# Two more transposed tiles per block copied by ScalarE, and VectorE's small work regrouped, in a two-layer graph network on one core

## What is computed

```python
# layer 0, h = relu(layernorm(x)), adj is 2048 x 2048, int32, 0 or 1
mask = (adj > 0)
deg = sum(mask, axis=1)
agg = mask @ h / max(deg, 1)
combined = concat([h @ W_self + b_self, agg @ W_nb + b_nb])
x = x + relu(combined @ W_comb + b_comb)
# layer 1, h = relu(layernorm(x)): five gated steps that use adj and adj.T
a_in, a_out = adj @ (state @ in_W.T + in_b), adj.T @ (state @ out_W.T + out_b)
...
out = x + tanh(state @ o1_W.T + o1_b) @ o2_W.T + o2_b
```

## Time and profile before

| | |
|---|---|
| three runs | 1233.97, 1235.68, 1235.68 us; median 1235.68 us |
| the profiled execution | 1233.81 us, of which the span of its instructions is 1232.0 us |
| TensorE busy | 1221.4 us, 99% of the span |
| VectorE busy | 759.4 us, 62% |
| ScalarE busy | 285.0 us, 23% |
| granted TensorE clock, mean | 0.998 of full speed |
| TensorE idle between 50 and 135 us, blocks two to four | 2.0 us |

### The profile page before, as it was taken

How to read it: one execution, slowest core, us unless ns; L and a number is a source line. 1 busy time by engine, 2 the same in 40 slices (tenths; PEclk the granted TensorE clock), 3 DMA queues, 4 the chain that set the end, 5 groups by cost and what they waited for, 6 DMA issues and landing times.

```text
span 1232.0 us, 12870 instructions
## 1 busy us (share of the span) xinstructions
PE 1221.4 (99%) x4872; PEld 590.6 (48%) x4872; DVE 759.4 (62%) x1276; ACT 285.0 (23%) x556; POOL 15.4 (1%) x15
## 2 busy tenths in 40 slices
PE   8999999999999999999999999999999999999998
PEld 5666654444444444444444444444444444444445
DVE  6677744787985464487357339726825864662674
ACT  5756200022322021033112113301202230120121
POOL 4000000000000000000000000000000000000000
PEclk9999999999999999999999999999999999999999
DMA  9454643960008604800740660192085039015202
GB/s 330 159 166 172 241 186 126 351 248 0 1 34 317 229 1 159 302 18 34 284 160 0 228 250 1 39 357 82 1 299 179 1 132 332 14 66 207 90 1 69
DMA packets 44507, 180.61 MB, mean 147 GB/s; under 512 B 3490, under 2 KB 13475, under 8 KB 29347
## 3 DMA queue, kind: packets, MB, share of 16 engines
q1 hardware_dynamic: 43440, 176.04, 39.5%
q0 software_dynamic: 720, 3.67, 0.8%
q10 hardware_dynamic: 290, 0.14, 0.0%
HBM read 144.71 MB, written 35.13 MB: 146 GB/s over the span
## 4 chain that ended last, share of the span: by engine, by line
PE 86%; DVE 3%; issue 1%; ACT 0%; DVEq 0%
PE bank L347 84%; PE bank L517 1%; DVE LF L1199 0%; DVE GR L1346 0%; DVE first_GZ L1346 0%; DVE first_GH L1319 0%; DVE first_GZ L1349 0%; DVE GR L1349 0%; DVE ST L1322 0%; DVE u_buf L1383 0%; DVE GR L1303 0%; PE bank L467 0%; ACT GR L951 0%; DVE H L1095 0%; DVE AT L1052 0%
## 5 line engine op out<-in xcount | busy, mean ns | idle before, releaser
L347 PE MATMUL bank<-slot,LF 128*128 128x512 f16 x1792 | 389.4, 379 | 0.0
L347 PEld LDWEIGHTS bank<-slot,LF 128*128 128x128 f16 x1792 | 175.3, 98 | 210.1 <-issue 2.3
L347 PE MATMUL bank<-X,W 128*128 128x512 f32 x384 | 180.5, 592 | 0.0
L347 PE MATMUL bank<-XT,W 128*128 128x512 f32 x288 | 135.3, 592 | 0.0
L347 PEld LDWEIGHTS bank<-X,W 128*128 128x128 f32 x384 | 72.5, 190 | 88.0 <-issue 86.9
L347 PE MATMUL bank<-AT,SN 128*128 (+1 forms) x256 | 97.0, 379 | 0.0
L347 PE MATMUL bank<-A,SN 128*128 (+1 forms) x256 | 97.0, 379 | 0.0
L1245 DVE TENSOR_TENSOR u_buf<-bank,m_buf 128x512 f32<-128x512 f32 x16 | 11.1, 691 | 134.0 <-PE bank L347 134.0
L347 PEld LDWEIGHTS bank<-XT,W 128*128 128x128 f32 x288 | 54.7, 190 | 68.9 <-issue 68.2
L767 ACT ACTIVATE m_buf<-bank 128x512 f32<-128x512 f32 x46 | 27.4, 595 | 231.9 <-PE bank L347 231.9
L347 PE MATMUL bank<-DR,work 128*128 128x512 f16 x256 | 67.1, 386 | 1.8 <-DVE DR L1063 1.6
(11 more groups left out here) (217 smaller groups left out, 1420.5 us busy)
## 6 DMA issues: line engine op xcount, KB each, us to landing
slot<-quad_d SPq DMA_DIRECT2D x112, 1024.0 KB, 5.1
WG<-in_adj SPq DMA_DIRECT2D x32, 512.0 KB, 4.2
quad_d<-AT SPq DMA_DIRECT2D x12, 1024.0 KB, 5.0
quad_d<-A SPq DMA_DIRECT2D x12, 1024.0 KB, 8.6
quad_d<-spare SPq DMA_DIRECT2D x4, 1024.0 KB, 4.0
SN<-in_x SPq DMA_DIRECT2D x2, 1024.0 KB, 10.4
x_d<-SN POOLq DMA_DIRECT2D x4, 512.0 KB, 3.2
x1o<-x_d SPq DMA_DIRECT2D x1, 2048.0 KB, 8.4
```

The lines of the kernel that those rows point to most:

```text
L347: return pe.matmul(o, l, r, start=start, stop=stop, skip_group_check=again)
```

## The change

One list, `ACT_MOVES`, says which tiles ScalarE moves: the even ones as before, and in blocks two to four also tiles 3 and 11 of the block. VectorE moves the rest. So six of the 64 tiles change engines. All counts of the two semaphores `at_act` and `at_dve` are taken from the list (`moved_by`). `residual` gets a first and a last tile in place of a half: two tiles in turn 2 as before, one in turn 4, one in turn 5. `row_stats` of the first two tiles goes from turn 5 to turn 3.

```diff
+ACT_MOVES = [i for i in range(NT * NB) if i % 2 == 0 or (i >= NT and i % NT in (3, 11))]
...
+        def moved_by(i):
+            on_act = sum(k <= i for k in ACT_MOVES)
+            return (at_act, on_act) if i in ACT_MOVES else (at_dve, i + 1 - on_act)
...
                 if i >= 3:
-                    if i % 2 == 1:
-                        pe.wait_ge(at_act, (i - 3) // 2 + 1)
-                    else:
-                        pe.wait_ge(at_dve, (i - 3) // 2 + 1)
+                    by, count = moved_by(i - 3)
+                    pe.wait_ge(by, count)
...
-                if i % 2 == 0 and i:
+                if i in ACT_MOVES and i:
                     move_adj(i)
...
-                if i % 2 == 0:
-                    dve.wait_ge(at_act, i // 2 + 1)
-                else:
-                    dve.wait_ge(at_dve, i // 2 + 1)
+                by, count = moved_by(i)
+                dve.wait_ge(by, count)
...
-            def residual(b, half):
-
-                for q in (2 * half, 2 * half + 1):
+            def residual(b, q0, q1):
+
+                for q in range(q0, q1):
...
-                if i % 2 == 1:
+                if i not in ACT_MOVES and i < NT * NB:
                     move_adj(i)
...
-                if i > NT and i % NT in (2, 4):
-                    residual(i // NT - 1, i % NT // 4)
+                if i > NT and i % NT == 2:
+                    residual(i // NT - 1, 0, 2)
+                if i > NT and i % NT in (4, 5):
+                    residual(i // NT - 1, i % NT - 2, i % NT - 1)
                 b = i // NT - 1
-                if i > NT and i % NT in (5, 6):
-                    row_stats(range(BT * b + 2 * (i % NT - 5), BT * b + 2 * (i % NT - 4)), BT * b)
+                if i > NT and i % NT in (3, 6):
+                    q = 2 * (i % NT // 6)
+                    row_stats(range(BT * b + q, BT * b + q + 2), BT * b)
```

More of the change, by code:

```diff
@@ L268, in _ @@
             sp.wait_ge(conv, 4 * NT)
-            sp.wait_ge(at_act, NT * NB // 2)
-            sp.wait_ge(at_dve, NT * NB // 2)
+            sp.wait_ge(at_act, len(ACT_MOVES))
+            sp.wait_ge(at_dve, NT * NB - len(ACT_MOVES))
             for p in range(2):
@@ L690, in _ @@
             pe.wait_ge(sn_lo, NB - 1)
-            pe.wait_ge(at_act, NT * NB // 2)
-            pe.wait_ge(at_dve, NT * NB // 2)
+            pe.wait_ge(at_act, len(ACT_MOVES))
+            pe.wait_ge(at_dve, NT * NB - len(ACT_MOVES))
             spread(0, 0, 2)
@@ L1141, in _ @@
             for half in range(2):
-                residual(NB - 1, half)
+                residual(NB - 1, 2 * half, 2 * half + 2)
             dve.wait_ge(conv, 4 * NT)
-            dve.wait_ge(at_act, NT * NB // 2)
+            dve.wait_ge(at_act, len(ACT_MOVES))
             v.tensor_reduce(degs[:, 0, :], degA[:, :, :], mybir.AxisListType.X, ALU.add)
```

## The result

| | before | changed |
|---|---|---|
| median of 20 runs | 1234.46 us (1232.24 to 1235.68) | 1231.38 us (1229.56 to 1235.57) |
| ratio, 95% interval | | 0.9981 (0.9976 to 0.9987) |
| profiled execution | 1233.81 us, span 1232.0 | 1229.56 us, span 1227.8 |
| start of mask product 16 to mask product 63 | 79.44 us | 76.89 us |
| from mask product 63 to the end | 1096.69 us | 1096.71 us |

A forecast was written before the change was run, and what follows sets the result against it. TensorE, busy 1221.4 of 1232.0 us, was taken as the bound, so only its waits could be won. 0.36 + 0.47 = 0.83 us a block, times three, gave 2.5: 1235.68 to 1233.2 us, range 1230.9 to 1235.5.

The forecast's parts named there:

- The bound: Blocks two to four: the change can touch only TensorE's mask waits at turns 20, 21 and 27, 3.2 us or 0.26%.
- the one at tile 32: Transposition of tile 32 comes 0.28 us late, held by a ScalarE conversion; this wait was expected to stay.
- Turns 20 and 21: Regrouping residual tiles and statistics starts turn 21 0.36 us earlier a block, of 0.59 lost; about 0.23 of wait stays.
- the lower bound: If residual tile 3 waits for the accumulator read (0.08), turn 21 is 0.1 us later and the sum 2.2.
- Turn 27: Moving tile 27 to ScalarE frees VectorE before the mask; the whole 0.47 us a block goes, 0.13 to spare.
- The move of tile 19: On ScalarE in turn 3 of block two, it starts at 57.24, takes 0.6 us in idle time and costs nothing.
- the rival that was built on it: A ScalarE move of tile 27 three times VectorE's 0.69 makes its mask 0.26 late; gain 1.7 us, 1234.0; chance 0.01.
- The delay of one conversion: ScalarE's conversion at 55.76 slips 2.1 us behind the move of tile 19; costs nothing, its second half frees the slot.
- the rival named the ring's slot: Slower: a late conversion frees the load ring's slot 2.08 us late, TensorE waits in blocks two and three; 1238.6; chance 0.05.
- The level of 1233.2: Forecast time of the whole kernel: the earlier median 1235.68 less 2.5 us; chance 0.70.
- the whole range: Time of the whole kernel, 1230.9 to 1235.5 us, set to cover two run levels 1.7 us apart and rivals at 1234.4.
- the bound of 0.2%: About 0.2%, 2.5 us, is what a measurement of this kernel can tell from no change.

The follow-up runs named there:

- the kernel with the copy in turn 15: Against the changed kernel, ScalarE copies the transposed second-layer input in turn 15, behind that turn's conversion, not in turn 14; turns 16 to 63 take 76.32 us, median 1231.04.
- the run with tile 11 alone: Against the changed kernel, only tile 11 of a block goes to ScalarE, tile 3 stays on VectorE; turns 16 to 63 take 76.88 us, median 1231.28, ratio 0.9972.

## Why the prediction was right

**The bound.** It was said that no more than TensorE's waits could be won, 3.2 us, and that they are best read from start to start. The 2.55 us of the stretch, in TensorE's starts and nowhere else, bear that out. Of the list of waits two readings were off. Its wait of 0.3 us for a conversion was taken for the one at tile 32; it lies at 21.88 us, ahead of the stage's first mask product, and the 0.28 at tiles 32 and 48 are too short for the list. That they are waits for a conversion is shown by the kernel with the copy in turn 15, where they went. And the masks were to count about three times in the list after; none of the three that are left is in it.

**Turns 20 and 21.** Forecast: 0.36 a block, with a wait of 0.23 left. From turn 19 to 21 it was 2.97 and is 2.60: 0.37, with 0.22 left. The residual tile starts together with the accumulator read, so the value that was taken was the right one and the lower bound, 0.1 less, was not needed.

**Turn 27.** Forecast: the whole 0.47, with 0.13 to spare. Both measured, 1.66 to 1.19 and 0.13.

**ScalarE.** The move of tile 19 was put 0.43 behind its transposition and measured 0.42 behind (55.13 to 55.55). The move of tile 20 came at 56.75, 0.44 after its transposition at 56.31, so it slipped by 0.02. The move of tile 27 took 0.58. The idle time ahead of the copy at 74.22 shrank by 0.37, where the prediction had at most 0.13 come out of it: counted from turn 16, the copy starts 0.85 earlier, with TensorE's gain at both places, and ScalarE's work ahead of it ends only 0.48 earlier. The room of 1.19 was wide enough for that. In these blocks a move takes 592 ns on ScalarE and 689 ns on VectorE. The page "ScalarE: Activation LUTs" of the Trainium skill, section "Rules for kernel authors", gives its factor of about three for operations with one source in VectorE's 4x mode; this copy out of PSUM shows nothing of that factor, and the rival that was built on it fell with the move of 0.58.

**What was right for less than the given reason.** The delay of one conversion, ScalarE's of turn 20, by 2.1 us was taken at nothing because its ring slot is freed by the next one. It did cost nothing, but the ring was not the tight side. The conversion one turn earlier, which the change does not delay, had 2.08 us before TensorE wanted it, and the rival named the ring's slot where it should have named tile 20. That the wait for tile 19 stands behind this conversion and not ahead of it was not weighed. And the move of tile 19, counted as part of the change at no gain and no loss, could have been left out, as the run with tile 11 alone shows.

**The time.** Sum: 2.5 forecast, 2.3 by the ratio and 2.55 by the trace. The level of 1233.2 was 1.8 too high. It went by the median of three runs, 1235.68; 20 runs of the same kernel have 1234.46, and the rest is the mix of clocks in the first 55 us. The median lies below the forecast's own range of 1232.5 to 1233.9, and 0.5 inside the lower end of the whole range, which had been set that low for the scatter. That the time fell into the range is owed to this width; that the mechanism is right is shown by the starts. The ratio of 0.9981 lies just inside the bound of 0.2% where the forecast lay just on it, so by that bound it came out the same, which had 0.45, and not faster, which had 0.49.

## What to carry to other kernels

Where one engine is 99% busy, read its timeline from start to start against the undisturbed pitch: that found 1.3 us a block in blocks two and three, where the list of waits showed 0.5. Ask of each wait in a list where it lies before it is put down to a stage. Ahead of a time-critical instruction on an in-order engine, put ready work before an instruction that has to wait, not behind it; that order alone was worth 0.7 us here, against 1.1 for the regrouping as it was made. And when an effect is a fifth of a per cent, compare a stretch of the trace that holds the edit and check that the rest is unchanged, for the clock of the first microseconds moved single executions by more than the change.

## What the runs showed of the hardware

TensorE's granted clock went from full to half near 30 us in some executions and not in others, with the same instructions up to there: for 3.4 us in three of ten profiles, for 6.8 us in two, not at all in five. In one of the two it fell although TensorE had been busy without a gap from 6.3 us on. Of the changed kernel, executions at full clock took 1229.6 to 1230.5 us and those at a mean of 0.997 or less 1232.8 to 1235.6. A piece of 48 passes with one output column each made it happen in 11 of 11 runs. A conversion was seen by TensorE 0.77 us after it started, a mask 0.35 us after, and a transposition by the copying engines 0.42 us after its start. Wherever these rows were read, before and after, they agreed to 0.02 us.
